# VectorE's sum of a unit issued one first product later, in a two-layer graph kernel on 8192 nodes

## The reference, cut to what matters

```
score_par = sigmoid(t @ w_par[:128] (rows) + t @ w_par[128:] (columns) + b_par)
score_chi = sigmoid(t @ w_chi[:128] (rows) + t @ w_chi[128:] (columns) + b_chi)
support   = (adj.T * score_chi) @ t + (adj * score_par) @ t        # t: tangent of x, 8192 x 128
x         = layernorm(x + proj(expmap0(support)))
```

## Time and profile before

| | |
|---|---|
| median of 3 runs | 2195.22 us (2194.65 to 2196.01) |
| the profiled execution | 2197.59 us, of which the span of the trace is 2195.8 us |
| busy share of the span | PE 91%, DVE 88%, POOL 61%, ACT 60% |
| mean share of the 16 DMA engines, mean rate | 374 GB/s over the span |
| the three-slot stage, units 195 to 511 | from about 1370 us to 2173 us of the span |

### The profile page before, as it was taken

How to read it: one execution, slowest core, us unless ns; L and a number is a source line. 1 busy time by engine, 2 the same in 40 slices (tenths; PEclk the granted TensorE clock), 3 DMA queues, 4 the chain that set the end, 5 groups by cost and what they waited for, 6 DMA issues and landing times. The chain is left out here.

```text
span 2195.8 us, 18377 instructions
## 1 busy us (share of the span) xinstructions
PE 2006.1 (91%) x5072; PEld 898.2 (41%) x5072; DVE 1929.8 (88%) x1872; ACT 1318.1 (60%) x1508; POOL 1340.9 (61%) x639
## 2 busy tenths in 40 slices
PE   7999999999999998999999878898888888889886
PEld 3444444444444444444444333343333333334333
DVE  5667777988989989999999989999898998989896
ACT  0001324354464454454453588988989988989996
POOL 0000304535455455644544677999998998999996
PEclk9999999999999999999999978999999999999998
DMA  9988979989989988989989998999999999999993
GB/s 337 361 285 290 408 285 356 406 340 382 381 333 409 408 337 363 394 338 348 422 329 362 421 399 332 422 420 421 421 406 421 421 417 403 421 420 391 399 391 144
DMA packets 128453, 820.37 MB, mean 374 GB/s; under 512 B 14880, under 2 KB 27488, under 8 KB 31328
## 3 DMA queue, kind: packets, MB, share of 16 engines
q1 hardware_dynamic: 113392, 799.06, 90.6%
q10 hardware_dynamic: 14960, 20.13, 2.7%
HBM read 814.88 MB, written 4.26 MB: 373 GB/s over the span
## 5 line engine op out<-in xcount | busy, mean ns | idle before, releaser
L550 POOL TENSOR_TENSOR chi<-chi,ring 128x1024 f32<-128x1024 f32 x326 | 835.3, 2578 | 623.5 <-ACT chi L758 569.4
L1257 PE MATMUL ps<-keys,xtA 128*128 128x512 f32 x2048 | 982.4, 611 | 138.9 <-DVE keys L1052 111.0
L1182 PE MATMUL ps<-ring,xA 128*128 128x512 f32 x2048 | 917.3, 598 | 32.4 <-DMA ring<-in_g_blk 16.2
L775 ACT ACTIVATE ps<-scores,prcr 128x1024 f32<-128x1024 f32 x492 | 544.2, 1106 | 395.1 <-DVE keys L1052 378.3
L1257 PEld LDWEIGHTS ps<-keys,xtA 128*128 128x128 f32 x2048 | 377.2, 193 | 684.6 <-issue 653.0
L937 DVE TENSOR_TENSOR dsum<-dsum,ring 128x2048 f32<-128x2048 f32 x240 | 590.2, 2459 | 33.8 <-DMA ring<-in_g_blk 28.1
L1182 PEld LDWEIGHTS ps<-ring,xA 128*128 128x128 f32 x2048 | 387.9, 192 | 515.5 <-issue 487.9
L1052 DVE TENSOR_TENSOR keys<-ps,chi 128x1024 f32<-128x1024 f32 x426 | 521.6, 1224 | 87.4 <-issue 35.2
L758 ACT ACTIVATE chi<-scores,prcr 128x1024 f32<-128x1024 f32 x426 | 483.9, 1136 | 15.9 <-DMA scores<-plcl_d 7.8
L1043 DVE TENSOR_TENSOR ps<-ps,ring 128x1024 f32<-128x1024 f32 x348 | 425.5, 1223 | 44.5 <-ACT ps L775 37.8
L550 POOL TENSOR_TENSOR chi<-chi,xA 128x1024 f32<-128x1024 f32 x79 | 186.2, 2375 | 18.8 <-ACT chi L758 18.8
(11 more groups left out here) (122 smaller groups left out, 823.9 us busy)
## 6 DMA issues: line engine op xcount, KB each, us to landing
ring<-in_g_blk SPq DMA_DIRECT2D x443, 1024.0 KB, 8.6
ring<-in_a_cols SPq DMA_DIRECT2D x190, 1024.0 KB, 10.1
xA<-in_a_cols SPq DMA_DIRECT2D x51, 1024.0 KB, 11.7
xA<-in_g_blk SPq DMA_DIRECT2D x44, 1024.0 KB, 9.9
scores<-in_a_cols SPq DMA_DIRECT2D x15, 1024.0 KB, 12.0
scores<-in_g_blk SPq DMA_DIRECT2D x15, 1024.0 KB, 10.1
scores<-plcl_d ACTq DMA_DIRECT2D x22, 512.0 KB, 10.5
xA<-in_x_g ACTq DMA_DIRECT2D x64, 64.0 KB, 10.3
```

The source lines that it names most:

```text
L550: pool.tensor_tensor(out=chi(n), in0=chi(n), in1=half(t, n), op=ALU.mult).then_inc(m2_ready, 1)
L775: act.activation(dst, scores[:, row, 0, :], ACT.Sigmoid, bias=prcr[:, 2 * jt:2 * jt + 1]).then_inc(p_ready, 1)
L1182: ins = pe.matmul(Y[:, h * BANK:(h + 1) * BANK], xA[:, tile * D:(tile + 1) * D], t[:, tt * BP + h * BANK:tt * BP + (h + 1) * BANK], start= ...
L1257: ins = pe.matmul(outp[:, h * BANK:(h + 1) * BANK], xtA[:, jt * D:(jt + 1) * D], keys(n)[:, h * BANK:(h + 1) * BANK], start=begins, stop=i ...
```

## The change

From unit 195 on (`SLOT_THREE`) DVE's sum of unit n - 1 is issued after the first product of unit n, and no longer ahead of it. At unit 195 only the first product is issued, and the last sum stands behind the loop. All other engines, all buffers, the slot rotation and all waits stay as they are, and no instruction is added or removed.

```
@@ the loop of VectorE @@
                 first_product(n)
-                key(n)
+                if n < SLOT_THREE:
+                    key(n)
+                elif n > SLOT_THREE:
+                    key(n - 1)
+            key(UNITS - 1)
             k = NPAN - 1
```

## The result

The changed kernel takes 2229.57 us (median of 4 runs, 2225.71 to 2232.20), the kernel before 2195.61 us (median of 4). The ratio is 1.0153, with a 95% interval of 1.0135 to 1.0170: 34 us slower. The forecast was 2218 us, slower, with a range of 2204 to 2238. Direction and range held; the loss is half again as large as the 22.6 us of the sum.

What follows compares the result with a forecast made beforehand. POOL's pace (18.6 us per eight units) was taken as the bound, with a 17.56 us loop under it growing to 19.35; 3.8 + 13.8 + 5 = 22.6 us on the median 2195.22 gave 2218 us, range 2204 to 2238.

Steps and rivals of the forecast that it cites:

- the 22.6 us of the sum: Added time from unit 195 on: 3.8 us for units 195 to 231, 13.8 for three stretches, 5 at the end.
- part 1: DVE's sum no longer reads the first product ahead of it: 1.13 us instead of 1.25, 0.12 less a unit.
- The last rival: DVE's step from first product to sum stays at 1.25 us, loop 19.95 us, 2238 us in all; chance 7%.
- part 2: Sum waits for the next unit's sigmoid; nine DVE steps make the apart-unit loop 19.35 us, 0.75 over POOL's 18.6.
- parts 3 and 4: Lent slots before table loads: interval 23.45 us, before 19.83; own blocks at PE's pace, 1.4 us more.
- C(366): Start of ACT's line 758 sigmoid for unit 366; such starts, four units after an apart unit, mark the intervals.
- part 5: DMA and SP: loads stay early with all of it slower, and no transfer is added.
- The sum over C(310) to C(382): 72 units of the late stage added interval by interval: 189.7 us, 4.6 more than the 185.15 before.
- the two intervals behind a panel's start: Units 310 to 318, with table loads and early panel's evacuation, 22.6 us; 318 to 326, line 775 waiting, 20.7 us.
- waits of the sum for PE: Sign of a failed forecast: such waits (`kt_used`) appearing in the profile after; no size given.
- The three stretches of 72 units: Late-stage stretches between units 231 and the final 58, priced at 4.6 us more each, 13.8 together.
- The last 58 units: End of the stage, with an own block, a root's table loads and three smooth groups: about 5 us more.

Runs made afterwards that it cites:

- e5: Changed kernel with ACT's line 775 sigmoid issued ahead of line 758 for units four after an apart unit; 2213.40 us, ratio 1.0068.
- e9: Kernel before, with only ACT's two sigmoids swapped for units four after an apart unit; 2202.77 us, ratio 1.0017.
- e1: Changed kernel, but at each apart unit the previous unit's sum goes ahead of the first product; 2213.05 us, ratio 1.0064.
- e6: Changed kernel, but the sum goes first again at own units and at b+5, b+7 and b+17; 2218.65 us, ratio 1.0086.
- e7: Changed kernel, but sum first at apart units, own units, b, b+5, b+7 and b+17; 2200.90 us, ratio 1.0009.
- e4: Changed kernel with no apart units; 2218.32 us, against 2212.63 us for the old order with no apart units.
- e2: Changed kernel, but the sum goes ahead of the first product of the unit four after each apart unit; 2230.15 us, ratio 1.0143.
- e8: Kernel before, with the late sum only for units b+12 to b+27, without apart and own units; 2188.42 us, ratio 0.9955.
- e10: Kernel before with the late sum only at b+12 to b+27, plus ACT's two sigmoids swapped four units after apart units; 2192.00 us, ratio 0.9967.

## Why the forecast was right, and where it was off

- **The bound.** GpSimd's pace with a loop through the apart units just under it: right. Before, 18.62; after, 19.38 with the loop above it, as worked out.
- **The step of 1.13 us** (part 1): right. In the trace of after, 275 of the 282 sums from unit 195 on start 1.12 to 1.14 us behind the first product of the next unit. The last rival, 1.25 us, is out. By that, the trace of after disagrees with the rule of the Trainium skill named in part 1 where it is taken to hold for every pair; the first of the two sections also says that a next operation that is not held starts earlier, and with that the 1.13 us agree.
- **The sum behind the next sigmoid** (part 2): right, shown by e5, which moves nothing but that sigmoid, by e9, where the same move gains nothing, and by e1. Its share of the cost is 15.5 to 16.7 of the stage's 31.2 us (e5, e1).
- **Lent slots and own blocks** (parts 3 and 4): right in kind, and their own intervals as forecast (23.46 us for 23.45; the sum of 375 comes 28.27 us after C(366), for 28.1). But undoing them gives 14 us, 9 by the stage, not 20; two intervals of e6 lose 1.4 and 1.8 us instead, each with a stretch at a granted clock of 0.50.
- **DMA** (part 5): right, the list of waits of the stage has none for a load.
- **The size.** 31.2 us in the stage against 22.6. The sum over C(310) to C(382) is 191.4 us (1669.37 to 1860.75), 189.7 in the forecast, 185.15 before. Six of the eight terms are within 0.4 us: 334 to 342 is 19.38 (19.35), 342 to 350 23.46 (23.5), 350 to 358 20.67 (20.5), 358 to 366 20.59 (21.0), 366 to 382 41.67 (41.5), 326 to 334 20.44 (20.6). The terms that were too small are the two intervals behind a panel's start, 23.55 (22.6) and 21.62 (20.7).

In the first, first product 311 and its sum come 7.31 and 10.72 us after C(310), as forecast (7.3 and 10.7). What is late is TensorE. PE of the kernel after, and below it the same place of the kernel before:

```profile
1679.18 5.37 PE L1261 MATMUL ps<-keys,xtA 128*128 128x512 f32 x8 [2.91 <-DVE keys L1052]
1680.00:1683.00 3.00, 3.00 (x4) 0.96 (x3) 3.00 (x6) 2.81 (x3) 3.00 (x3) 0.50 1.03 412
1685.67 5.42 PE L1261 MATMUL ps<-keys,xtA 128*128 128x512 f32 x12 [1.11 <-ACT acc L803]
1692.92 1.15 ACT L758 ACTIVATE xA<-scores,prcr 128x1024 f32<-128x1024 f32 x1 [0.59 <-PE ps L1267]
...
1667.54 1.96 PE L1257 MATMUL ps<-keys,xtA 128*128 128x512 f32 x4 [1.53 <-DVE keys L1052]
1667.50:1669.50 2.00, 1.96 (x4) 0.68 (x4) 1.72 (x2) 2.00 (x3) 2.00 (x2) 1.00 0.99 401
...
1856.97 7.11 PE L1257 MATMUL ps<-keys,xtA 128*128 128x512 f32 x12 [2.32 <-ACT acc L803]
```

The late sum of 310 leaves TensorE idle for 2.91 us, where it was idle for 1.53 before. Behind that the granted clock is 0.50, the lower of its two levels (1.2 GHz), and the eight matmuls of 310 and 311 take 5.37 us, 1.7 more than the 3.67 of eight at the full clock. ACT's evacuation waits for them, and from PE's next start to C(318) it is 7.25 us, as before. The forecast priced TensorE at its full clock throughout. C(382) to C(390) is 23.55 us as well, with 5.37 us for the same eight matmuls; there the kernel before has a stretch at 0.50 too (1858.1 to 1861.4 us, the last row), and takes 23.38 us where it takes 21.69 from C(310). First product 314, an apart one, waits 0.97 us for PE's products of 311 and holds up sum 313 behind it. The forecast named waits of the sum for PE as a sign of its failing; as the 7.25 us are unchanged, this wait took no part.

In the second interval, for units 322 and 326 of the kernel after:

```profile
1704.96 1.12 ACT L775 ACTIVATE ps<-scores,prcr 128x1024 f32<-128x1024 f32 x1 [1.03 <-DVE keys L1052]
1714.54 1.14 ACT L758 ACTIVATE xA<-scores,prcr 128x1024 f32<-128x1024 f32 x1
```

ACT's short normalisations of 0.48 us stand between the sigmoids, so that those of line 775 of 318 to 321 come 2.47 us apart and VectorE has to go at that pace. Line 775 of 322 starts 12.04 us after C(318), not 11.5, and sum 321 at 14.39, not 13.8. Then C(326) shows no wait for PE: ACT is itself late with the units in front, and starts it 7.23 us after sum 321, not 6.88.

The three stretches of 72 units come to 6.7, 6.2 and 5.8 us, not 4.6, and the part ahead of C(238) to 4.2 and not 3.8. The last 58 units cost 8.4 us and not 5, and half of that is one interval. Unit 454, ACT and PE of the kernel after:

```profile
2050.42 1.15 ACT L758 ACTIVATE xA<-scores,prcr 128x1024 f32<-128x1024 f32 x1 [0.16 <-PE ps L1267]
2052.93 1.12 ACT L775 ACTIVATE ps<-scores,prcr 128x1024 f32<-128x1024 f32 x1 [1.36 <-DVE keys L1052]
2062.06 7.07 PE L1261 MATMUL ps<-keys,xtA 128*128 128x512 f32 x12 [3.45 <-DVE keys L1052]
2062.10:2065.40 3.30, 3.30 (x4) 1.44 (x5) 3.30 (x6) 3.30 (x5) 3.30 (x2) 0.50 0.97 397
```

Line 775 of 454 waits for sum 452, the table loads follow it, and PE is idle for 3.45 us and then at a granted clock of 0.50. The interval is 25.14 us, 20.88 before. The forecast has no figure of its own for it. At the same place behind 304, line 775 of 310 needs no such wait, since C(310) itself comes late.

- **Open.** 4.7 us of the stage remain in e7 with every named place undone. Part is PE's queue of e1 (18.77 for 18.62), and the largest losses lie in the three intervals at a granted clock of 0.50. No run holds the clock, so its share of the 31 us isn't known, nor whether the late sum brings the falls about: in the kernel before, waits of 1.53 and 2.32 us were followed by the full clock behind C(310) and by a clock of 0.50 behind C(382). That the sum of two undone parts makes e7 does not show that there is no third. In e4 the split between own blocks and panel ends was read from the traces and not tried alone.

## What to carry to other kernels

An instruction that is moved behind another inherits all that the other waits for, on every queue that feeds it: here a sum took over a sigmoid's place behind a sigmoid that waits for TensorE. Look for the loop that comes back to the same buffer, add its starts, and compare with the pace of the busiest engine; here a loop of 17.56 us under a pace of 18.6 cost nothing, and one of 19.38 cost 0.8 us each time round. A step taken out of such a loop is worth only as much as the next link allows: here 0.6 of 1.13 us (e1) and 0.2 (e2). A cheaper step on an engine is worth having only in the stretches where that engine is the late one (e8). Where a change lengthens a wait of TensorE, look at the granted clock behind that wait before its matmuls are priced.

## What the runs showed of the hardware

Two VectorE operations of 128 x 1024 in float32 start 1.12 to 1.14 us apart when the second doesn't read the first's result, whichever of the two lines they are (275 of 282 pairs of the kernel after), and 1.24 to 1.26 us when it reads the result and waits for it by a semaphore (228 of 283 pairs of the kernel before). The 0.12 us belong to reading and waiting together: no run has one without the other. Issuing late sums where VectorE was late gave 10 us in e8.

TensorE's granted clock fell to 0.50 for short stretches in the middle of this stage, in the kernel before as after, and eight matmuls then took 5.37 to 6.50 us for 3.67 at the full clock. In the stretches shown TensorE had been idle for 2.91 to 3.45 us just before, but behind C(382) of the kernel before the fall followed waits of 1.53 and 2.32 us. GpSimd's product of unit 195 started 6 us apart in e9 and e10 (1369.9 and 1376.1 us).
